# Row statistics finished inside the projections, two pairs of blocks joined, and expert results added up in DRAM

## The reference

```python
x = x + L0_xattn(ctx, layernorm(x), mask)      # phase 1
x = x + L0_attn(layernorm(x))                  # phase 2
x = x + L0_ffn(layernorm(x))                   # phase 3: product-key experts
x = x + L1_xattn(layernorm(x), ctx)            # phase 4
x = x + L1_attn(layernorm(x))                  # phase 5: selective state space
x = x + L1_ffn(layernorm(x))                   # phase 6: 2 of 8 experts per row
def _layernorm(x, axis=-1, eps=1e-05):
    m = jnp.mean(x, axis=axis, keepdims=True)
    v = jnp.var(x, axis=axis, keepdims=True)
    return (x - m) / jnp.sqrt(v + eps)
```

```python
y_t = jnp.einsum('bdn,bn->bd', state, C_t) + D * x_t
y = y * _silu(z)
return y @ W_out
...
topk_scores, topk_idx = jax.lax.top_k(logits, TOP_K)
topk_gates = jax.nn.softmax(topk_scores, axis=-1)
...
h = jax.nn.relu(jnp.einsum('bsd,df->bsf', x, w1) + bb1)
y = jnp.einsum('bsf,fd->bsd', h, w2) + bb2
return (acc + y * c[..., None], None)
```

## Time and profile before

| measure | value |
|---|---|
| median of 3 runs | 2870.3 us (2867.86 to 2873.23) |
| the profiled execution: its time / its span | 2871.1 us / 2869.3 us |
| instructions | 79950 |
| PE busy | 2556.5 us (89%) |
| DVE busy | 2049.3 us (71%) |
| ACT busy | 1447.5 us (50%) |
| POOL busy | 651.4 us (23%) |
| mean DMA rate | 45 GB/s |

### The profile page before, as it was taken

The page is one execution under the profiler, slowest core; times in us unless marked ns, Lnnn a source line. Parts: engine busy times, 40 slices in busy tenths (PEclk is TensorE's granted clock), DMA queues, the critical chain, the costliest instruction groups (busy, mean ns, idle before and its releaser), DMA issues. The chain is left out here.

```text
span 2869.3 us, 79950 instructions
## 1 busy us (share of the span) xinstructions
PE 2556.5 (89%) x29927; PEld 1900.8 (66%) x29928; DVE 2049.3 (71%) x4862; ACT 1447.5 (50%) x3939; POOL 651.4 (23%) x931
## 2 busy tenths in 40 slices
PE   8899999799799999999989999978777776869995
PEld 4688887455578888888865666643433333769995
DVE  6688886576668888888856887855699999532223
ACT  4355444355335555555537888832777773013331
POOL 5555554111100000000002333310222221024442
PEclk9999999899999999999999999989699999769998
DMA  5322221000220000000001111113000001441113
GB/s 123 88 69 68 71 71 41 1 1 0 85 101 3 3 3 2 2 2 2 2 29 42 44 48 48 44 32 125 0 1 1 1 1 59 180 177 37 37 37 107
DMA packets 86969, 128.29 MB, mean 45 GB/s; under 512 B 22877, under 2 KB 67357, under 8 KB 82558
## 3 DMA queue, kind: packets, MB, share of 16 engines
q1 hardware_dynamic: 80782, 113.18, 12.2%
q0 software_dynamic: 3744, 10.23, 1.1%
q10 hardware_dynamic: 2256, 2.16, 0.2%
HBM read 105.67 MB, written 19.87 MB: 44 GB/s over the span
## 5 line engine op out<-in xcount | busy, mean ns | idle before, releaser
L1454 PE MATMUL s_ps<-s3e_xT,s_down 128*128 128x128 f32 x2048 | 256.0, 279 | 0.0
L1454 PEld LDWEIGHTS s_ps<-s3e_xT,s_down 128*128 128x128 f32 x2048 | 244.8, 194 | 13.8 <-issue 8.1
L1465 PE MATMUL s_ps<-s_up,s3e_gh 128*128 128x256 f32 x1024 | 241.6, 380 | 3.1 <-DVE s3e_gh L1623 2.2
L1465 PEld LDWEIGHTS s_ps<-s_up,s3e_gh 128*128 128x128 f32 x1024 | 185.3, 190 | 25.1 <-DVE s3e_gh L1623 2.6
L1513 ACT ACTIVATE s3e_gh<-s_ps 128x512 f32<-128x512 f32 x128 | 76.5, 598 | 233.3 <-PE s_ps L1465 211.4
L2917 ACT ACTIVATE s6e_hT<-s_ps,s_b 128x128 f32<-128x128 f32 x312 | 84.8, 382 | 189.8 <-PE s_ps L2890 189.8
L2556 DVE SCALAR_TENSOR_TENSOR s5c_fresh<-s_ps,s5c_state 128x1024 f32<-128x1024 f32 x124 | 151.5, 1221 | 11.3 <-PE s_ps L2510 4.5
L1499 ACT ACTIVATE s3e_apart<-s_number,s3e_picksT 128x128 f32<-128x128 f32 x512 | 156.1, 388 | 1.6
L2890 PEld LDWEIGHTS s_ps<-s6e_xT,s6e_w 128*128 128x128 f32 x1248 | 149.6, 197 | 5.5 <-ACT s6e_xT L2921 3.5
L2890 PE MATMUL s_ps<-s6e_xT,s6e_w 128*128 128x128 f32 x1248 | 150.1, 280 | 2.9 <-ACT s6e_xT L2921 2.9
L1876 PE MATMUL s_ps<-s4a_wv,s4a_cT 128*128 128x256 f32 (+1 forms) x512 | 151.5, 404 | 1.1 <-PEq L1704 1.1
(11 more groups left out here) (438 smaller groups left out, 6271.0 us busy)
## 6 DMA issues: line engine op xcount, KB each, us to landing
s4a_cT<-ctxR SPq DMA_DIRECT2D x64, 257.0 KB, 2.6
s_w<-p_w SPq DMA_DIRECT2D x16, 1024.0 KB, 13.5
s_bcx<-ctx SPq DMA_DIRECT2D x64, 192.0 KB, 2.5
s_bcT<-ctxT SPq DMA_DIRECT2D x64, 192.0 KB, 2.9
s_down<-p_down SPq DMA_DIRECT2D x1, 4096.0 KB, 22.4
s_up<-p_up SPq DMA_DIRECT2D x1, 4096.0 KB, 31.6
s_silu_z<-s5p_sz SPq DMA_DIRECT2D x4, 1024.0 KB, 4.5
s_skipped<-s_xi SPq DMA_DIRECT2D x4, 1024.0 KB, 3.9
```

Of the source, the lines that this page charges most:

```text
L1454: mm = pe.matmul(banks[:, H_BANK + i % 2, tok(e)], lhsT=down[:, k, i * CH + e, :], rhs=xT[:, c.u, k, :], start=k == 0, stop=k == KT - 1)
L1465: mm = pe.matmul(banks[:, Y_BANK, 0:D], lhsT=gh[:, o.u, e, :], rhs=up[:, e, :], start=e == 0, stop=e == NE - 1)
```

## The change

The statistics (`row_stats`, with `g.stats`) become a shared object `g.norm`, which works in four groups of four tiles. `project_out` and the new `turn_and_project` finish three groups inside their loops, at t = 5, 9 and 13, and POOL takes each group's power beside them; the next phase's start has only the last group (in phase 2 ahead of its first norm, in phase 5 behind the first pair of norms, in phase 6 behind the first four). Phases 3 and 4 start without such a projection before them and do all four groups there, each norm behind its group.

```diff
+    def moments(self, dve, link, i):
+
+
+        ts = slice(i * self.GROUP, (i + 1) * self.GROUP)
+        for t in range(ts.start, ts.stop):
+            last = dve.bn_aggr(self.mv[:, t, :], self.stats[:, t, :])
         link(last)
-    for t in range(NT):
-        last = dve.bn_aggr(mv[:, t, :], stats[:, t, :])
-    link(last)
-    return dve.tensor_scalar(var[:, :], mv[:, :, 1], eps, None, ALU.add)
-
-
-def project_out(nc, g, name, banks, OT, wo, bias=None, kt=KT, gate=None):
+        return dve.tensor_scalar(self.var[:, ts], self.mv[:, ts, 1], LN_EPS, None, ALU.add)
+
+    def roots(self, pool, i):
+        ts = slice(i * self.GROUP, (i + 1) * self.GROUP)
+        return pool.tensor_tensor(self.rstd[:, ts], self.var[:, ts], bc(self.half[:], P, self.GROUP), ALU.pow)
...
+        def _(pool):
+            pool.memset(n.half[:], -0.5).then_inc(half_ready, 1)
+            pool.wait_ge(half_ready, 1)
+            for i in range(n.GROUPS - 1):
+                pool.wait_ge(stat_ready, i + 1)
+                n.roots(pool, i).then_inc(rstd_ready, 1)
+            pool.wait_ge(rstd_ready, n.GROUPS - 1)
...
+                if t > n.GROUP and t % n.GROUP == 1:
+                    link.settle()
+                    n.moments(dve, link, t // n.GROUP - 1).then_inc(stat_ready, 1)
```

At the end of phase 5, the product of skip and D moves to ACT at the end of the scan, the gates are asked for in the scan too (two DMAs of 2 MB, behind the skip's, into the buffer that decay_first used), and `turn_back` and `project_out` become one block:

```diff
+            sp.wait_ge(turned, 4 * (S - 2) - 4)
+            for h in range(2):
+                sp.dma_start(gt[:, h, :, :], gate.rearrange("k p t -> p k t")[:, :, h * (T // 2):(h + 1) * (T // 2)]).then_inc(gate_loaded[h], 16)
...
+            act.wait_ge(skip_loaded, 16)
+            for k in range(DT):
+                act.activation(dt[:, k, :], dt[:, k, :], ACT.Identity, scale=vec[:, k, D_AT:D_AT + 1])
...
+                for k in range(by_pool.start, by_pool.stop):
+                    pool.wait_ge(taken, h * GROUPS + 2 * k + 2)
+                    pool.tensor_tensor(OT[:, k, hs], OT[:, k, hs], gt[:, h, k, :], ALU.mult).then_inc(gated_by_pool, 1)
...
+            for i in range(GROUPS):
+                turn(0, i)
+            for i in range(OUT):
+                turn(1, i)
+            for t in range(NT):
+                if t % (NT // 2) == 0:
+                    h = t // (NT // 2)
+                    pe.wait_ge(gated_by_pool, 2 * h + 2)
+                    pe.wait_ge(gated_by_vector, h + 1)
+                after(pe, added, t - OUT + 1)
                 for k in range(DT):
...
+                if t < GROUPS - OUT:
+                    turn(1, OUT + t)
```

In phase 6, `route` stores X to a DRAM tensor `sums` behind the weights and makes a list with two columns for each tile (place and gate share; 78 columns at L2744's successor). `experts` multiplies y by its share on DVE, and the scatter adds into `sums`; `combine` is gone, and `out` is copied from `sums`:

```diff
+            for j in range(2):
+                ins = dve.tensor_tensor(put[:, j, :, 0, :], bc(tile_no[:].unsqueeze(1), P, NT, LISTED), bc(tile_f[:, j, :].unsqueeze(2), P, NT, LISTED), ALU.is_equal)
+            dve.tensor_tensor(away[:], bc(home[:, 0:NT].unsqueeze(1), P, 2, NT), row_f[:], ALU.subtract)
+            link(ins)
+            for j in range(2):
+                ins = dve.tensor_tensor(put[:, j, :, 1, :], put[:, j, :, 0, :], bc(gates[:, j, :].unsqueeze(2), P, NT, LISTED), ALU.mult)
+            link(ins)
+            for j in range(2):
+                dve.tensor_tensor(put[:, j, :, 0, :], put[:, j, :, 0, :], bc(away[:, j, :].unsqueeze(2), P, NT, LISTED), ALU.mult)
             for i in range(NT // NG):
...
+                    if isinstance(o.b, int) and o.b == 0:
+                        pool.wait_ge(v["sums_begun"], 16 * 4)
                     pool.wait_ge(y_ready, o.b + 1)
                     after(pool, told, o.b)
                     after(pool, stored, 16 * o.b)
                     pool.tensor_tensor(one[:, 2:3], one[:, 0:1], one[:, 0:1], ALU.mult).then_inc(told, 1)
...
-                    pool.indirect_dma_start(results, bass.IndirectOffsetOnAxis(to[:, o.u, :], 0), y[:, o.u, :], None).then_inc(stored, 16)
+                    pool.indirect_dma_start(sums, bass.IndirectOffsetOnAxis(to[:, o.u, :], 0), y[:, o.u, :], None, compute_op=ALU.add).then_inc(stored, 16)
...
+            act.wait_ge(stored, 16 * LISTED)
+            for i in range(1, NS, 2):
+                copied(act, i)
...
-                    dve.tensor_tensor(y[:, o.u, :], banks[:, Y_BANK, 0:D], b2[:, bass.ds(e, 1), :].rearrange("p e d -> p (e d)"), ALU.add).then_inc(y_ready, 1)
+                    dve.tensor_tensor(y[:, o.u, :], banks[:, Y_BANK, 0:D], b2[:, bass.ds(e, 1), :].rearrange("p e d -> p (e d)"), ALU.add).then_inc(y_read, 1)
+                    dve.wait_ge(y_read, o.b + 1)
+                    dve.tensor_scalar(y[:, o.u, :], y[:, o.u, :], shares[:, bass.ds(o.b, 1)], None, ALU.mult).then_inc(y_ready, 1)
```

More of the change, by code:

```diff
@@ L886, in phase2 @@
         fourmask = sb("fourmask", [P, R4])
[L887 to L888 removed]
+        n = g.norm
         xn = sb("xn", [P, U, D])
@@ L2597, in _, with turn @@
         @block.tensor
         def _(pe):
-            for q in range(QUADS):
-                for k in range(DT):
-                    i = q * DT + k
-                    after(pe, added, i - 7)
-                    for half in range(2):
-                        mm = pe.transpose(banks[:, i % 8, tok(half)], xi[:, q % 2 * 2 + half, q // 2 * C + k * P:q // 2 * C + (k + 1) * P], g.ident[:])
-                    mm.then_inc(turned, 1)
+            def turn(h, i):
+                k, part = divmod(i, 2)
+                if h:
+                    pe.wait_ge(taken, i + 1 if i < OUT else GROUPS + i - OUT + 1)
+                for j in range(4):
+                    q = 4 * part + j
+                    mm = pe.transpose(banks[:, bank_of(h, i), tok(j)], xi[:, q % 2 * 2 + h, q // 2 * C + k * P:q // 2 * C + (k + 1) * P], g.ident[:])
+                mm.then_inc(turned, 1)
@@ new lines, in _ @@
+            for i in range(GROUPS):
+                take(0, i)
+            gate(0)
+            for i in range(OUT):
+                take(1, i)
+            for t in range(NT):
+                dve.wait_ge(product, t + 1)
+                dve.tensor_tensor(X[:, t, :], X[:, t, :], banks[:, OUT + t % OUT, 0:D], ALU.add).then_inc(added, 1)
+                if t < GROUPS - OUT:
+                    take(1, OUT + t)
+                if t:
+                    ins = statistics(t - 1)
+                    if t % n.GROUP == 0:
+                        link.mark(ins)
+                if t > n.GROUP and t % n.GROUP == 1:
+                    link.settle()
+                    n.moments(dve, link, t // n.GROUP - 1).then_inc(stat_ready, 1)
+                if t == GROUPS - OUT:
+                    gate(1)
@@ L2647, in route @@
     E, LISTED = v["E"], v["LISTED"]
-    slots, gates, listed, homes, owner, rows = (v[n] for n in "slots gates listed homes owner rows".split())
+    slots, listed, homes, shares, owner, rows, sums = (v[n] for n in "slots listed homes shares owner rows sums".split())
     SHIFT = P.bit_length() - 1
```

350 lines of the change are left out of this document (141 added, 209 removed).

## The result

| | before | changed |
|---|---|---|
| median | 2870.53 us (2867.86 to 2873.23, 4 runs) | 2835.53 us (2834.54 to 2838.19, 4 runs) |
| span of the profiled execution | 2869.3 us | 2832.7 us |

The ratio is 0.988, 95% interval 0.9865 to 0.9896: 35.0 us faster, where 30.7 were forecast (2839.6, range 2829 to 2855).

The account below looks back on a forecast made before the run. TensorE is busy 89% of the span, so edits inside a phase pay only where it waits. Gains summing to 30.7 us took the profiled 2871.1 to 2840.4; with the median 0.8 lower, forecast 2839.6 us, range 2829 to 2855.

Parts of the forecast that it names:

- A: Seam of phases 1 to 2: the first norm no longer waits for POOL's power; 3.8 us gained, bounds 2.0 and 4.0.
- D: Seam of phases 4 to 5: first pair of norms goes ahead of the last group's aggregations; 4.4 us gained, bounds 3.0 and 4.4.
- B: Start of phase 3: the first norm needs only one group, the long power goes; 0.4 us gained, bounds 0 and 1.2.
- C: Start of phase 4: it waits for its loads, which the change leaves; 0 us gained, bounds 0 and 0.4.
- E: End of phase 5: projections start earlier, about 9.1 us behind the first transpose; 7.6 us gained, bounds 5 and 9.
- F: Route: earlier start 3.6, less 1.7 for list operations and 1.0 for a later first gather; 0.9 us gained, bounds −3 and 3.
- Experts: Experts' 39 tiles: extra multiply off TensorE's path, adding scatter's landing of 3.6 us fits the 7.17 period; 0 us.
- G: End of the kernel: copies ahead of POOL's drain replace combine's loads and stores; 13.6 us gained, bounds 9.3 and 18.0.
- The rival of the clock: Shorter seams keep TensorE's clock up at A, D and F and in the list product: 2829 to 2835 us; chance 0.08.

Follow-up runs that it names:

- again: The changed kernel itself run once more, with no edit: 2835.7 us (4 runs).
- plain: The changed kernel with a plain scatter to the sums instead of an adding one, so the addition is left out: 2834.67 us (one run).
- twice: The changed kernel with each tile's adding scatter done a second time, behind the first one's landing: 2912.59 us (one run).
- old_p5: The changed kernel with the end of phase 5 (turning back and projecting) as before, grouped statistics kept: 2844.92 us (4 runs).
- both: The changed kernel with X stored and adds made in the output, empty places dropped, no copies, X's stores after the first two gathers: 2829.16 us.

## Why the prediction was right, step by step

*A and D* (3.8 and 4.4): 3.87 and 4.36. Both as priced. The power of four columns took 1.17, so tile 2 never waited. *B* (0.4): 0.66, but not as I argued. I read the idle of 1.19 as "behind the power of sixteen"; in phase 3 the power was split into 4 and 12 columns before, and the first norm waited for the short one, as it does now:

```profile
L1220 POOL TENSOR_TENSOR s_rstd<-s_var,s_half x2: 1006/1635/2264, 774.1 to 775.1; 128x4 f32<-128x4 f32 x1, 128x12 f32<-128x12 f32 x1
```

What went are 12 of the 16 aggregations ahead of that power: the first norm starts 1.95 us behind the first aggregation instead of 2.57. That the size fits is luck. *C* (0): 0.46, which is scatter: the stage took 6.9 to 7.4 in all the kernels with the new code, and 7.3 before.

*E* (7.6): 6.64, of which 0.7 are missing in turning (9.81 instead of 9.1) and 0.2 in projecting. The first takes came 0.86 apart, not 0.61: each waited 0.17 for TensorE's four transposes, at a clock of 0.50, where I had 0.154 us a transpose from a stretch at 0.60; the eighth take ended 7.3 behind the first transpose, not 6.6. The windows of the changed kernel:

```profile
2427.00:2429.00 2.00, 2.00 (x11) 2.00 (x11) 1.66 (x3) 0.00 (x0) 1.56 (x1) 0.50 0.00 0
2429.00:2431.00 2.00, 2.00 (x17) 2.00 (x16) 1.70 (x3) 0.00 (x0) 2.00 (x2) 0.80 0.00 0
```

VectorE's gate and what came behind it were as priced. The projecting had +1.5 for transposes and -1.5 for the clock, and measured +0.22; its granted clock was 1.00, before 0.95.

*F* (0.9): the gain of 3.6 measured 3.63, by two errors that offset each other: the 1.6 us to rb's landing count from its issue's start, so that the 0.43 of the issue was added twice, and in the changed kernel rb is issued 0.33 later behind phase 5's last product. The six list operations took 1.68 more (1.7), the product 0.07 (0). The term that was mis-sized is the first gather, 1.0 forecast, bounds 0 and 2: it was 2.67, and 1.99 in `again`. The stores' 2 MB lengthen DMA traffic that started at the barrier, and TensorE arrives 2 us earlier. With it F is -0.8 (-0.4 by `again`): from phase 5's last product to the first gathered tile it took 62.4 us before and 63.2 after, though route starts 3.6 earlier. The window at the gathers shows what it waits for (changed kernel):

```profile
2520.00:2523.00 3.00, 0.00 (x0) 0.00 (x0) 1.44 (x3) 0.00 (x0) 2.11 (x3) 0.50 1.08 384
2523.00:2526.00 3.00, 0.00 (x0) 0.00 (x0) 0.00 (x0) 0.00 (x0) 1.31 (x3) 0.50 0.70 241
```

*Experts* (0): 0.00, shown by `plain` and `twice` to be the slack of 7.2 us and not a free add.

*G* (13.6): 15.35, in 4 terms. From the last product to the last scatter's issue end +0.96 (0.45: the issue too is 0.6 longer); the landing 2.3 behind it (3.6); the copies 9.9 us from SP's wake to the last landing (1.6 + 9 = 10.6); the tail 1.0 (1.3). The landing was mis-sized. My upper bound added a gather's 2.8, which the view counts from the issue's start, to a scatter's 2.2, which I had counted from the issue's end. From its issue's start the last scatter landed in 3.87, the plain one before in 3.2.

The lettered stages come to 30.6 where the sum was 30.7. So near a hit is luck: E and F came out 1.0 and 1.7 lower than forecast, G 1.8 and C 0.5 higher. By the second profile the lettered stages come to 31.6. The recorded range isn't worked out rightly either: the bounds' distances halved give 2835 to 2847, whole 2830 to 2854, and not "2829 to 2850".

The rest of the 35.0, 4.4 us (2.2 in `again`, whose medians differ by 33.8), is in stages that I had put at nothing. In the first pair of profiles phases 2, 3 and 5 and the first tile are 6.6 shorter, at places where the code is the same (but for phase 5's first norms and what ACT and SP do at its end), and `again` shows bodies of one kernel 0.3 to 1.6 apart from one execution to the next. Phase 3 has both its values under the same code, the slower one in seven variants. Phase 5's 1.4 goes with the change, as shown above. The first tile's 2.5 (15.81 before, 12.9 to 13.9 in the changed kernel and ten variants or repeats, 15.59 in old_p5) is the granted clock: TensorE's work on the first and the second tile took 6.54 and 5.42 us before, and 5.63 and 3.84 in the changed kernel:

```profile
2547.16:2553.70 6.54, 6.54 (x34) 6.51 (x34) 1.23 (x1) 0.00 (x0) 1.80 (x1) 0.57 0.07 20
2556.33:2561.75 5.42, 5.42 (x34) 5.42 (x35) 0.00 (x0) 0.00 (x0) 0.23 (x1) 0.69 0.08 24
2528.40:2534.03 5.63, 5.63 (x34) 5.61 (x34) 1.23 (x1) 0.00 (x0) 1.81 (x1) 0.66 0.09 23
2536.68:2540.52 3.84, 3.84 (x34) 3.84 (x35) 0.00 (x0) 0.00 (x0) 0.23 (x1) 1.00 0.12 34
```

Why the clock dipped there in the kernel before and in old_p5, and in none of the other eleven profiles, stays open; the kernel before was profiled once.

The rival of the clock, 0.08, didn't come about at the places that it named: the list product ran at 0.50 as before, and at the start of phase 2 the clock fell 2 us behind the restart instead of lying low from it:

```profile
513.20:515.00 1.80, 1.32 (x4) 0.66 (x5) 0.00 (x0) 0.38 (x1) 0.72 (x1) 0.98 0.02 5
515.00:517.00 2.00, 2.00 (x4) 0.80 (x3) 0.00 (x0) 0.00 (x0) 0.00 (x0) 0.50 0.00 0
```

Its idea, that shorter seams give back clock, has a part in the result all the same: phase 5's 1.4 us, and perhaps the first tile's 2.5.

## What to carry to other kernels

At a barrier, finish there only the last group of a reduction whose inputs are made in a loop before, and put the wait for its slow step where the value is first read: the smaller group gave two thirds of each seam here and the moved wait one third. A step that makes an engine ready earlier at a place where DMA traffic began at a barrier can give its time back at the next load, here 1.9 to 2.6 of 3.6 us; look at what the queues hold until then. A stage whose code is the same can still follow the edit, as phase 5 did here: only the profiles of all variants side by side tell that from scatter. An adding scatter that each tile waits for is free while its landing fits the tile's period, and only the last one is paid; where the sum is the output, add into the output.

## What the runs showed of the hardware

- An adding scatter of 128 rows of 1 KB landed 4.2 us after its issue's start in the median of the changed kernel and 3.8 in that of `twice`, a plain one 3.0 (`plain`).
- A copy of 2.1 MB from DRAM to DRAM, in eight DMAs on two queues, ran at 295 to 361 GB/s in the six windows of 1 us from 2823 to 2829, and took 9.9 us from the first issue to the last landing. The Trainium skill ("DMA: Bandwidth & Descriptors", section "Latency and other measured facts") gives 207 to 214 GB/s per direction for copies of 128 x 16 KiB tiles between HBM tensors (at row pitches of 512 KiB, and of 4 MiB plus 4 KiB); by it the data alone would take 9.8 us, an estimate. Here it flowed for 7 to 8 us, so the trace doesn't agree: its rate in those windows is about one and a half times the page's.
- POOL's drain at a block's exit lasted 8.2 to 8.3 us around an adding scatter and 7.8 around a plain one, and ended 4.2 us (before) and 5.2 us (`both`) behind SP's passing of the landing.
- A power of 128x4 took 1.00 to 1.32 us on POOL (20 in the changed kernel, median 1.01), one of 128x12 2.26 and one of 128x16 2.9.
